# A Mamba and expert block: the gate's residual added on TensorE and copied by ScalarE, the second FFN layer one step later, the product with C of state 26 on VectorE, and the first two scans between two experts' weights

## The reference

```python
xn = _layernorm(x, axis=-1)
# selective scan, once forwards and once on the reversed tokens, d_inner 256, 16 states each
delta = softplus(dt_proj(x_proj(xn)[:32]) + dt_proj_b)
h[t] = exp(delta[t] * A) * h[t - 1] + delta[t] * B[t] * xn[t]
y[t] = sum over the 16 states of C[t] * h[t], + D * xn[t]
# FFN with the expert `sel` of the row
h = gelu(xn @ W1[sel] + b1[sel])
out = (h @ W2[sel] + b2[sel]) @ Wo + bo
g = silu(xn + 0.3 * out)
return x + (y_forward + y_backward) * g
```

## Time and profile before

| | before |
|---|---|
| median of 3 runs | 3116.98 us (3115.43 to 3118.45) |
| the profiled execution: its time | 3118.2 us |
| its span in the trace | 3116.4 us |
| VectorE (DVE) busy | 3021.6 us, 97% |
| GpSimd (POOL) busy | 3013.3 us, 97% |
| ScalarE (ACT) busy | 2940.6 us, 94% |
| TensorE (PE) busy | 2489.1 us, 80% |
| mean granted TensorE clock | 0.958 of full speed |

### The profile page before, as it was taken

The page is one execution under the profiler, slowest core; times in us unless marked ns, Lnnn a source line. Parts: engine busy times, 40 slices in busy tenths (PEclk is TensorE's granted clock), DMA queues, the critical chain, the costliest instruction groups (busy, mean ns, idle before and its releaser), DMA issues. The chain is left out here.

```text
span 3116.4 us, 49216 instructions
## 1 busy us (share of the span) xinstructions
PE 2489.1 (80%) x15990; PEld 1970.9 (63%) x15990; DVE 3021.6 (97%) x1995; ACT 2940.6 (94%) x5242; POOL 3013.3 (97%) x1486
## 2 busy tenths in 40 slices
PE   7878878878778888788787788887788887887886
PEld 6666656666656666566666566666666665666665
DVE  3999999999999999999999999999999999999999
ACT  5899999999999999999999999999999999999995
POOL 3899999999999999999999999999999999999997
PEclk9999999999999999999999999999999999999998
DMA  5543334444334444344433444443444433444331
GB/s 174 151 134 116 125 119 130 143 125 119 118 123 141 135 124 123 111 131 143 130 120 119 127 128 140 127 124 111 128 139 134 126 120 114 131 144 130 107 122 55
DMA packets 273364, 394.17 MB, mean 126 GB/s; under 512 B 45003, under 2 KB 119508, under 8 KB 273108
## 3 DMA queue, kind: packets, MB, share of 16 engines
q1 hardware_dynamic: 273108, 391.03, 41.1%
HBM read 348.98 MB, written 25.18 MB: 120 GB/s over the span
## 5 line engine op out<-in xcount | busy, mean ns | idle before, releaser
L480 POOL TENSOR_TENSOR bx<-dx,b_sb 128x1024 f32<-128x1024 f32 x576 | 1362.9, 2388 | 10.2 <-DVE hs L861 9.5
L861 DVE TENSOR_TENSOR_SCAN hs<-decay,bx 128x1024 f32<-128x1024 f32 x576 | 1308.7, 2277 | 8.7 <-ACT decay L682 4.3
L468 POOL TENSOR_TENSOR hc<-hs,c_sb 128x1024 f32<-128x1024 f32 x480 | 1135.7, 2376 | 22.6 <-DVE hs L861 21.1
L1091 PE MATMUL y<-ident,hc 128*128 128x128 f32 x8192 | 1068.6, 277 | 36.0 <-DVE hc L840 36.0
L1091 PEld LDWEIGHTS y<-ident,hc 128*128 128x128 f32 x8192 | 942.0, 143 | 148.5 <-DVE hc L840 106.0
L861 DVE TENSOR_TENSOR_SCAN hs<-decay_sb,decay 128x1024 f32<-128x1024 f32 x448 | 1004.7, 2266 | 11.8 <-issue 10.5
L682 ACT ACTIVATE decay<-delta,rate 128x512 f32<-128x512 f32 x1152 | 745.6, 684 | 38.8 <-DVE hs L861 35.9
L594 ACT ACTIVATE dxb<-dxT,btok 128x256 f32<-128x256 f32 x1792 | 759.2, 503 | 0.3 <-PE decay L1066 0.3
L1066 PE MATMUL decay<-ident,dxb 128*128 128x128 f32 x3584 | 477.2, 276 | 244.9 <-DVE hs L861 212.8
L840 DVE TENSOR_TENSOR hc<-hs,c 128x1024 f32<-128x1024 f32 x544 | 649.6, 1194 | 1.3 <-issue 0.7
L1066 PEld LDWEIGHTS decay<-ident,dxb 128*128 128x128 f32 x3584 | 396.5, 141 | 401.3 <-issue 259.1
(11 more groups left out here) (125 smaller groups left out, 2050.8 us busy)
## 6 DMA issues: line engine op xcount, KB each, us to landing
b_sb<-b_scratch SPq DMA_DIRECT2D x576, 256.0 KB, 3.3
c_sb<-b_scratch SPq DMA_DIRECT2D x480, 256.0 KB, 3.5
xin<-in_L_attn_x_dram SPq DMA_DIRECT2D x32, 512.0 KB, 6.6
w_sb<-in_L_ffn_W_dram SPq DMA_DIRECT2D x32, 512.0 KB, 3.4
w2o_sb<-w2o_scratch SPq DMA_DIRECT2D x32, 512.0 KB
xres<-in_L_attn_x_dram SPq DMA_DIRECT2D x32, 512.0 KB, 5.4
out_dram<-og SPq DMA_DIRECT2D x32, 512.0 KB, 4.3
dbc<-high SPq DMA_DIRECT2D x64, 128.0 KB, 2.3
```

The source lines that it names most:

```text
L468: nc.gpsimd.tensor_tensor(hc[:, s % RING, :, :], hs[:, s % HSLOTS, :, :], c_sb[:, i % CRING, :].unsqueeze(1).broadcast_to([P, DT, T]), ALU ...
L480: nc.gpsimd.tensor_tensor(bx[:, i % RING, :, :], dx[:, g, :, :], b_sb[:, i % BRING, :].unsqueeze(1).broadcast_to([P, DT, T]), ALU.mult).th ...
L861: V.tensor_tensor_scan(hs[:, s % HSLOTS, :, :].rearrange("p k t -> p (k t)")[:, u], factor.rearrange("p k t -> p (k t)")[:, u], data.rearr ...
L1091: ins = M(yps[:, c, k * P:(k + 1) * P], hc[:, s % RING, k, c * P:(c + 1) * P], ident[:, :], start=False, stop=(s == ADDED[-1]), is_transpo ...
```

## The change

- `gate_input` moves from VectorE to ScalarE. VectorE computed 0.3 * bank + `xn` in one instruction. Now W2·Wo and the bias are scaled by 0.3 when they are prepared, TensorE adds `xn` to the bank by one more matmul for each quarter (identity as the weights, float32, 128x256), and ScalarE copies the bank to `zz`. It stands at steps 4 and 6 of ScalarE's program, where before it stood at steps 3 and 6 of VectorE's.
- The pairs of parts of `ffn_out` move, for rows 1 to 31, from steps 31, 32, 34 and 35 to steps 32, 33, 35 and 36.
- Step 26 leaves `POOL_C`: GpSimd makes 14 products with C in a row and VectorE 18, and one row of C less is loaded.
- Ahead of row 0: scans 0 and 1 stand between the experts' copies on VectorE, the products of experts 6 and 7 go to other PSUM banks, decays 0 to 3 are made earlier, expert 7 is copied ahead of the GELU, loads of B, C and of the next row's tokens are issued later, and the first `broadcast_c` earlier. Stored W2·Wo has its rows in another order.

```diff
-    FFN_OUT, GATE = (31, 31, 32, 32, 34, 34, 35, 35), (35, 38)
-    FFN_OUT_FIRST, GATE_FIRST = (33, 33, 34, 34, 36, 36, 37, 37), (36, 38)
+    FFN_OUT, GATE = (32, 32, 33, 33, 35, 35, 36, 36), (36, 38)
+    FFN_OUT_FIRST, GATE_FIRST = (34, 34, 35, 35, 36, 36, 37, 37), (36, 38)
-    POOL_C, C_LAG, ADD_LAG = (2, 4, 5, 7, 9, 10, 11, 12, 16, 18, 20, 22, 24, 26, 27), 4, 2
+    POOL_C, C_LAG, ADD_LAG = (2, 4, 5, 7, 9, 10, 11, 12, 16, 18, 20, 22, 24, 27), 4, 2
...
-        w2T_ps, w2o_ps = y_bank, [[dps[a][:, h, :] for h in range(2)] for a in range(2)]
+        w2T_ps, w2o_ps = y_bank, [[y_bank[h] if e == NE - 1 else dps[min(e, NE - 3) % 2][:, h, :] for h in range(2)] for e in range(NE)]
...
+            def gate_input(row, v):
+                act.wait_ge(s_pf, row * UNITS + 12 + v)
+                if v == 0:
+                    wait(act, s_yg, row)
+                A(zz[:, 2 * v:2 * v + 2, :], fps[:, :].rearrange("p (c d) -> p c d", c=2), ACT.Copy).then_inc(s_zz, 1)
...
-                V.scalar_tensor_tensor(zz[:, 2 * v:2 * v + 2, :], fps[:, :].rearrange("p (c d) -> p c d", c=2), 0.3,
-                                       xn[:, 2 * v:2 * v + 2, :], ALU.mult, ALU.add).then_inc(s_zz, 1)
...
-                    ins = M(to, ones3[:, :], bias3[:, :], start=False, stop=True)
+                    M(to, ones3[:, :], bias3[:, :], start=False, stop=False)
+                    ins = M(to, ident[:, :], xn[:, c, :], start=False, stop=True)
...
+            act.wait_ge(s_w2oc, 2 * NE - 2)
+            make_decay(0, 0, 1)
             hidden(0, 2)
...
+            make_decay(0, 0, 2)
             hidden(0, 3)
+            make_decay(0, 0, 3)
+            copy_w2o(7, 0)
+            copy_w2o(7, 1)
             gelu(0)
             act.preload_act_table_set(exp_ln)
-            copy_w2o(7, 0)
-            copy_w2o(7, 1)
-            act.wait_ge(s_w2oc, 2 * NE)
-            make_decay(0, 0, 1)
...
-            for e in range(4, NE):
-                copy_w2T(e)
+            copy_w2T(4)
+            copy_w2T(5)
+            scan(0, 0)
+            copy_w2T(6)
+            scan(0, 1)
+            copy_w2T(7)
```

More of the change, by code:

```diff
@@ L365, in _ @@
             load_w2(3)
-            load_x(1)
             store_w2o(0)
@@ L370, in _ @@
             store_w2o(1)
-            for j in range(BRING - 1):
+            for j in range(2):
                 load_b(0, 0, j)
-            for j in range(C_AHEAD):
-                load_c(0, 0, j)
             load_w2(5)
@@ L384, in _ @@
             store_w2o(4)
+            for j in range(2, BRING - 1):
+                load_b(0, 0, j)
+            load_x(1)
             load_w2(7)
+            store_w2o(5)
             sp.wait_ge(s_biasc, 5)
             sp.dma_start(bias_dram, bias_part[:, :, :]).then_inc(s_biasst, 16)
-            for e in range(5, NE):
+            for j in range(C_AHEAD):
+                load_c(0, 0, j)
+            for e in range(6, NE):
                 store_w2o(e)
@@ L653, in drain @@
                     hidden(row, HIDDEN.index(s))
+                at = GATE if row else GATE_FIRST
+                if s in at:
+                    gate_input(row, at.index(s))
             def front(row, par, s):
@@ L676, in copy_w2o @@
                 act.wait_ge(s_w2o, 2 * e + h + 1)
-                A(w2o_st[a][:, 2 * h:2 * h + 2, :], w2o_ps[a][h][:, :].rearrange("p (j d) -> p j d", j=2),
-                  ACT.Copy).then_inc(s_w2oc, 1)
+                A(w2o_st[a][:, 2 * h:2 * h + 2, :], w2o_ps[e][h][:, :].rearrange("p (j d) -> p j d", j=2),
+                  ACT.Copy, scale=FFN_SCALE).then_inc(s_w2oc, 1)
             def decay_of(row, par, s, to, k):
@@ L724, in _ @@
             absolute(0, 0, 0)
[L725 to L726 removed]
             act.wait_ge(s_rv, 6)
             A(lexp[:, :], router_ps[0:NB, 384:384 + NE], ACT.Exp, bias=lneg[:, :], accum_out=lsum[:, :]).then_inc(s_ra, 1)
+            absolute(0, 0, 1)
             exp_abs(0, 0)
+            copy_w2o(3, 0)
+            log_one_plus(0, 0)
             absolute(0, 0, 2)
[L731 removed]
+            square(0, 0)
             copy_w2o(3, 1)
+            ratio(0, 0)
             absolute(0, 0, 3)
[L734 to L735 removed]
             copy_w2o(4, 0)
+            exp_abs(0, 1)
             copy_w2o(4, 1)
[L738 removed]
+            log_one_plus(0, 1)
+            act.wait_ge(s_rate, 1)
+            act.wait_ge(s_w2oc, 2 * NE - 6)
+            make_decay(0, 0, 0)
             copy_w2o(5, 0)
[L740 removed]
             copy_w2o(5, 1)
+            hidden(0, 0)
             square(0, 1)
[L743 removed]
+            hidden(0, 1)
             ratio(0, 1)
             copy_w2o(6, 0)
[L746 removed]
             copy_w2o(6, 1)
+            act.wait_ge(s_w2oc, 2 * NE - 2)
+            make_decay(0, 0, 1)
             hidden(0, 2)
[L749 to L751 removed]
+            make_decay(0, 0, 2)
             hidden(0, 3)
+            make_decay(0, 0, 3)
+            copy_w2o(7, 0)
+            copy_w2o(7, 1)
             gelu(0)
             act.preload_act_table_set(exp_ln)
[L755 to L758 removed]
             copy_dxT(0, 0)
@@ L771, in body @@
                     if s + DSLOTS < STEPS:
-                        if s + DSLOTS not in AHEAD.values() and (row == 0 or s + DSLOTS not in AHEAD_NEXT.values()):
+                        if row == 0 and s + DSLOTS < 4:
+                            pass
+                        elif s + DSLOTS not in AHEAD.values() and (row == 0 or s + DSLOTS not in AHEAD_NEXT.values()):
                             make_decay(row, par, s + DSLOTS)
@@ L928, in _ @@
             V.tensor_copy(bias_part[:, 2, :], bias_rest2[:, :]).then_inc(s_biasc, 1)
-            for e in range(4, NE):
-                copy_w2T(e)
+            copy_w2T(4)
[4 more added lines that the diff above has]
+            copy_w2T(7)
             def body(row, par, last):
                 for s in range(STEPS):
-                    scan(row, s)
+                    if row or s > 1:
+                        scan(row, s)
                     if s == 0 and row:
@@ L1076, in skip_term @@
             def skip_term(row, par, s):
-                if s == 0:
-                    wait(pe, s_yg, row)
+                if s == 0 and row == 0:
+                    pe.wait_ge(s_w2oc, 2 * NE)
+                elif s == 0:
+                    pe.wait_ge(s_yg, row)
                 for c, k in SKIP[s]:
@@ L1107, in times_wo @@
                 pe.wait_ge(s_w2Tc, 2 * e + h + 1)
-                wait(pe, s_w2oc, 2 * e + h - 3)
+                if e < NE - 1:
+                    wait(pe, s_w2oc, 2 * e + h - (3 if e < NE - 2 else 1))
                 for j in range(2):
                     for k in range(DT):
-                        ins = M(w2o_ps[e % 2][h][:, j * D:(j + 1) * D], w2T[e % 2][:, 2 * h + j, k, :], wo_sb[:, k, :],
+                        ins = M(w2o_ps[e][h][:, j * D:(j + 1) * D], w2T[e % 2][:, 2 * h + j, k, :], wo_sb[:, k, :],
                                 start=(k == 0), stop=(k == DT - 1))
@@ L1169, in _ @@
             M(bias_ps[0:NE, 0:D], ones_row[:, 0:NE], bo_row[:, :], start=False, stop=True).then_inc(s_bias, 1)
+            expand_delta(0, 0, 2)
+            times_wo(3, 1)
             turn_w2(4)
+            expand_delta(0, 0, 3)
             times_wo(4, 0)
@@ L1175, in _ @@
             times_wo(5, 1)
+            for k in range(DT):
+                ffn_in(0, 0, 0, k)
             turn_w2(6)
             for k in range(DT):
-                ffn_in(0, 0, 0, k)
+                ffn_in(0, 0, 1, k)
             times_wo(6, 0)
-            for k in range(DT):
-                ffn_in(0, 0, 1, k)
             times_wo(6, 1)
+            pe.wait_ge(s_biasc, 2)
+            broadcast_c(0, 0, 0)
             for k in range(DT):
@@ L1191, in _ @@
             turn_dx(0, 1, False)
-            pe.wait_ge(s_biasc, 2)
-            pe.wait_ge(s_ra, 5)
-            broadcast_c(0, 0, 0)
             pe.wait_ge(s_diag, DT)
```

22 lines of the change are left out of this document (7 added, 15 removed).

## The result

The changed kernel takes 3297.07 us (median of 4, 3296.14 to 3297.99) against 3116.74, a ratio of 1.0578 with a 95% interval of 1.0565 to 1.0591. Its profiled span is 3295.6 us against 3116.4, and its mean granted TensorE clock 0.929 against 0.958. The forecast was 3285.

A forecast was written before the change was run, and what follows sets the result against it. VectorE's written order sets the pace. Per row -0.04 - 0.27 + 3.7 + 1.64 + 0.7 = +5.7 us, times 31 is 177, less 5 is 172: 3290, median 3289, said as 3285; own range 3250 to 3325, chance 0.67.

The forecast's parts named there:

- TensorE's queue: Between product 0 and product 6 TensorE needs 18.2 us, VectorE 15.4, so VectorE stalls twice a row.
- Broadcast 3 to broadcast 6: TensorE's stretch between the broadcasts of C for steps 3 and 6: from 8.40 to 9.32 us.
- Stall A: VectorE's wait for the broadcast ahead of step 3's product: 1.38 us a row at full clock, 3.7 with slow clock.
- Stall B: VectorE's second wait, ahead of step 6's product with C: 1.64 us a row.
- The clock: After its gap TensorE starts at 1.2 GHz for 4.6 us, adding 2.3 us a row to the step 3 wait.
- The rival with a full clock: TensorE's clock stays at 2.4 GHz or rises at once: +3.2 us a row, 3211 us; chance 0.14.
- VectorE's own sum: VectorE loses two gates and gains one product of 1.12 us: -0.04 us a row, -0.31 with bank waits gone.
- The chain: ScalarE loses its slack behind the second gate copy; late decays widen the gap ahead of scan 13: +0.7 us a row.
- The start: Ahead of row 0, moved scans and an earlier expert 7 copy: -5 us once, bounds 0 and -12.
- The faster case: No stall, VectorE at its own sum, -0.31 us a row: 3102 us; chance 0.06.
- The case over 3325: ScalarE becomes a second bound or the clock is low 6 us each time: +1.5 us a row, 3335; chance 0.11.
- The last step: Final lowering of the forecast to 3285 us, since stalls in a chain can share slack counted twice.

The follow-up runs named there:

- run 1: Changed kernel with the second layer's pairs of parts back at steps 31, 32, 34 and 35: 3164.56 us.
- run 2: Changed kernel without the matmul that adds `xn` to the gate, so the gate lacks the residual: 3239.62 us.
- run 3: Changed kernel with the broadcast of C for step 3 issued at step 1, ahead of the second pair: 3295.35 us.
- run 4: Changed kernel with 32 idle transposes at the end of step 31, in TensorE's gap ahead of broadcast 1: 3243.68 us.
- run 7: Two kernels, each the changed one plus 32 idle transposes at step 31: state 26's product back on GpSimd, 3208.04 us; decay 9 ahead of the second gate copy, 3209.75.
- run 6: Changed kernel with decay 9 made at step 6, ahead of ScalarE's second gate copy: 3246.44 us.
- run 8: Of the change only the part ahead of row 0, scaled weights and row 0's places kept; gate on VectorE again: 3111.52 us against 3117.78 before the change.
- the faster version: The kernel keeping only the changed start, gate on VectorE: 3111.52 us; with 16 idle transposes ahead of the first pair at step 31: 3134.11.

## Why the prediction was right

**TensorE's queue.** Right, and shown three ways: taking the pair out of the queue (run 1), shortening the queue (run 2) and reordering it (run 3). Broadcast 3 to broadcast 6 was forecast as 9.32 us and took 1504.76 - 1495.45 = 9.31. Stall A at full clock was forecast as 1.38 us, and run 4 has 1.42. Stall B was 1.64 and is 1.46 + 0.12 = 1.58, a small part of it as a late scan 7 (which instruction holds that scan isn't shown).

**The clock.** 2.3 us a row forecast, 2.0 measured by run 4. The 2.3 is the average of three slow stretches of 3.0 to 6.0 us in other places, and the rows have two kinds, with 2.6 and 1.5 us: that their average came so near is in part luck. The sentence of the Trainium skill ("TensorE: Matmul & The Clock Gate", section "What's actually happening") that for modelling the ramp is under 1% of a typical kernel's span doesn't hold here: the low clock was worth at least 53 of 3297 us, 1.6%, since each row pays it again in the place without slack. The rival with a full clock (3211) was off by that and by the late decays.

**VectorE's own sum.** The product of state 26 is worth 1.1 us a row, as forecast (run 7, 35.6 us in 32 rows). That it shows only where the gap is filled wasn't foreseen.

**ScalarE.** The chain is the right one (run 6): it starts at the second copy and ends at scan 13. Its size was too small: 0.7 us was taken and 1.2 measured, just over its bound of 1.1; by run 7 it is 1.1. Two steps erred. One is the taking of a value below the 1.0 that its own count gave, on the hope that the wait for `xnT` would stay; that wait is gone. The other is the count up to decay 9, which put ScalarE (3.8 us from the start of broadcast 6) level with VectorE (3.85). It took 1507.82 + 1.32 - 1504.76 = 4.38: the copy started 0.39 us after the broadcast and not 0.05, and the normalising 0.69 after the copy and not 0.5. So scan 9 was already 0.46 late. The first copy cost nothing, as forecast.

**The start.** -5 us forecast; -6.8 at scan 13 of row 0 and about -6 in run 8.

**Busy times.** GpSimd's was to fall by 75 us and ScalarE's to rise by 36; they moved by -62 and +30. VectorE's rose by 15.6 instead of falling by 1. Most of that can be put down to the records: what follows a wait doesn't overlap with the instruction ahead, and four more waits in each of 31 rows are 10 us.

**The rivals.** The faster case needed TensorE's 18.2 us to shrink to 15.4; they grew. The case over 3325 needed more late decays; there were none behind scan 13. The last step, from 3290 down to 3285 for slack counted twice, went the wrong way: nothing was counted twice. That the sum before that step, 3289, came within 8 us has luck in it too: the clock's term was 0.3 us a row too large, ScalarE's 0.5 too small.

## What to carry to other kernels

An engine that is 80% busy can be the bound of a stretch: count what is queued on it between two handovers and set that against what its partner does between the same two, before asking for busy shares. Work that fills an engine's gap is free, and the same work one step later, behind the instruction that ends the gap, is paid in full, and with it the low clock that the gap leaves behind. Where a small gain doesn't arrive, look whether the clock moved, and repeat the comparison with the gap filled.

## What was not expected of the hardware

An edit that touches only ScalarE's order, and one that takes a single broadcast a row from TensorE, changed how long its clock stayed low. The wait ahead of product 3 was 3.4 us a row in the changed kernel, by turns 4.0 and 2.9, but 3.8 with a product moved to GpSimd and 2.9 with a decay made earlier, and one and the same kernel ran at 3269.9 once and at 3289.2 to 3291.4 three times. With 32 idle transposes in the gap (mean granted clock 0.961 instead of 0.929) both edits were worth what their counts said. The idle transposes help only where the gap is the one that counts: 16 of them in the faster version cost 23 us.
